# Two convolutions ahead: a convolution moved from a stage of its own into the loop over the queries

## The chip, the cores and the metric

The kernel runs on one core of one Trainium2 chip. The metric is the time of one execution on the device, in microseconds. Three runs of the kernel before gave 4277.91, 4282.75 and 4284.51 us; the median is 4282.75. One more execution was recorded by the hardware profiler.

## What is computed

The input x has 16 images of 256 channels and 64 x 64 pixels, in float32. Two layers follow one another, each added to its own input. Cut to what matters (B = 16, C = 256, N = 4096 tokens, nh = 8 heads of hd = 32):

```python
def layer0(x):                       # base_kernel [8, 32, 32, 3, 3]
    pooled = x.mean(axis=(2, 3))
    h = relu(pooled @ ap_w1.T + ap_b1)
    angles = tanh(h @ ap_w2.T + ap_b2) * (pi / 4)       # 8 a image
    w = rotate_bilinear(base_kernel, angles).reshape(B * C, 32, 3, 3)
    feat = conv2d(x.reshape(1, B * C, H, W), w, pad=1, groups=B * 8)
    m = relu(pooled @ meta_w1.T + meta_b1)
    return feat * sigmoid(m @ meta_w2.T + meta_b2)

def layer1(x):
    q, kv = xt @ Wq.T + bq, xt @ Wkv.T + bkv            # xt: tokens x 256
    q, k = ((relu(t) + 1e-6) / softplus(scale) for t in (q, k))
    q = q**3 / norm(q**3) * norm(q); k = k**3 / norm(k**3) * norm(k)
    z = 1 / (q . k.sum(tokens) + 1e-6)
    out = (q @ (k.T @ v)) * z                           # each head by itself
    out = out + depthwise_conv5x5(v) + dwc_b
    return (out @ Wproj.T + bproj).transpose(...)

x = x + layer0(group_norm(x))        # 32 groups of 8 channels
x = x + layer1(group_norm(x))
```

The weights of the convolution thus hang on the image: each image has its own eight angles, found from means over its pixels, and its own modulation of the channels.

## The kernel before

Each engine has its own program, written out by hand; semaphores tie them together (`wait_ge`, `then_inc`), and each engine does its instructions strictly in the order written. That order, and the order of the DMAs on SyncE (SP), is all that sets which work stands beside which. Matrices go through TensorE (PE) in pairs of float16 halves, a high one and a low one that holds the rest, in three products of four (`PASSES`).

An image b goes through these stages, in the function `batch` of each engine:

1. **Keys and values**, eight units of 512 tokens, each in two steps (`step_kv`): projection, the powers and norms of the keys, and the sum that makes the state of the attention. The change leaves it alone but for the small matmuls of `modulation`.
2. **Depthwise convolution**, `depthwise`: 32 channels of 9 matmuls each on PE, in four PSUM banks; ACT copies each one out (L1119). Beside it DVE takes the statistics of image b+2's pixels (`pixel_stats`, 16 BATCH_NORM_STATS), and ACT prepares the first three planes of image b+1 (`planes`, L1056: normalise in one pass, then set the borders to zero in six small ones).
3. **Convolution of image b+1**, `convolution`: eight groups of 32 channels (`GROUPS`), each in two halves of 512 columns (q = 0, 1), so 16 half groups, each of 12 matmuls (L1264). Half q goes to bank VA[q]. For a group, ACT makes the plane, DVE casts its high half (`high`), GpSimd (POOL) subtracts to get the low half. DVE then takes the bank, multiplies by the modulation and adds the residual (L792, in `conv_steps`), and takes the statistics for the second norm (L795); ACT adds the bias (`shift`), and SP stores the image x1 to memory. Between groups stand the small chains of image b+2's statistics: mean, deviation, angles. ACT ends them with `squash` (Tanh and Sigmoid, Sin), and POOL rotates the kernels in `rotation`, 27 chained operations.
4. **Queries' loop**, units u = 0 to 10, each in two steps p = 0, 1 (`step_q`). It is a pipeline: in step (u, p) PE does the projection of unit u (L1283), the transposes of the queries one step before (L1333), the attention of unit u-1 (L1342), the output projection of unit u-2 (L1361, h = 0 in bank PP and h = 1 in bank SM, both in step p = 1) and the transposes of the outputs (L1351). ACT does `squares`, `norms`, `sixths` (L1085), the copies of the transposed tiles (`transposed_q`, L1126; `high_out`, L1130). DVE does `floor_max` (L809), `ratio` (L820), `cube`, `denominators`, `inverses`, `quotients`, `low_out` (L899) and `finish` (L893). POOL adds the depthwise result to the quotients (L528). From u = 3 on, image b+1's attention inputs are prepared as well: ACT normalises (`attn_input`), DVE casts (L803), POOL subtracts. Units 3 to 7 have every one of these; unit 8 starts the keys of image b+1.

The body runs in a loop over images 0 to 13, then by itself for image 14 (no image b+2) and image 15 (nothing ahead). In front stands a prologue: loading and splitting of the weights, the statistics and the chain of image 0, its rotation, the convolution of image 0, its attention inputs, the first keys.

In the printed functions, L numbers are lines of the kernel before.

## Time and profile before

| | |
|---|---|
| median of three runs | 4282.75 us |
| profiled execution, its own time | 4280.34 us |
| its span, first to last instruction | 4278.5 us |
| PE busy | 3613.9 us, 84% of the span |
| DVE, ACT busy | 2916.5 us (68%), 2882.6 us (67%) |
| POOL busy | 1394.2 us, 33% |
| mean granted clock of PE | 0.971 of full speed |
| HBM traffic over the span | 113 GB/s |

PE is the busiest engine, and is named in 58% of the chain of work that ended last. A share of busy time is a mean over stages with different limits, so the rows below are taken stage by stage, from one image in the middle of the run (b = 1, with the convolution of image 2). In a window's row the columns are named; in a timeline's row, a bracket tells how long the engine was idle before the instruction and what released it. Engines: PE = TensorE, PEld = its weight loads, DVE = VectorE, ACT = ScalarE, POOL = GpSimd.

### The profile page before, as it was taken

What the parts mean: (1) busy time and instruction counts of PE and PEld (TensorE: products, weight loads), DVE (VectorE), ACT (ScalarE), POOL (GpSimd) and SP (SyncE); (2) the same over time, 40 slices, a digit from 0 to 9 for tenths busy, and PEclk for the clock granted to TensorE, in tenths of its full rate; (3) what the DMA queues carried; (4) which work ended last, traced back from release to release, by engine and by line L of the source; (5) the groups of instructions that cost most, each with busy time, mean ns of one, the idle gap of its engine ahead of it and who ended that gap; (6) DMA issues with size and microseconds to landing.
All of it is one profiled execution on the core that took longest, in us unless ns stands there. A gap on an engine that the chain in (4) does not pass through costs nothing.

```text
span 4278.5 us, 94152 instructions
## 1 busy us (share of the span) xinstructions
PE 3613.9 (84%) x26496; PEld 2725.6 (64%) x26496; DVE 2916.5 (68%) x7633; ACT 2882.6 (67%) x8141; POOL 1394.2 (33%) x1317
## 2 busy tenths in 40 slices
PE   0478898988889888898988889888898988889897
PEld 0265666757567575666757567675666757567686
DVE  6465767667576775867667576775857668585756
ACT  2366776767667676766767667676766767677675
POOL 0442522325143242513325143242513325142301
PEclk9989999999999999999999999999999999999999
DMA  4434434344443434444344442434444343432412
GB/s 161 135 95 149 131 116 126 109 131 126 132 132 95 139 107 140 131 122 123 112 126 126 141 135 89 135 116 129 130 131 121 105 132 118 150 111 81 129 40 69
DMA packets 558467, 516.39 MB, mean 121 GB/s; under 512 B 97296, under 2 KB 491664, under 8 KB 557712
## 3 DMA queue, kind: packets, MB, share of 16 engines
q1 hardware_dynamic: 557968, 510.53, 39.5%
q8 instruction: 217, 3.56, 0.4%
q14 instruction: 282, 2.31, 0.2%
HBM read 351.02 MB, written 134.22 MB: 113 GB/s over the span
## 4 chain that ended last, share of the span: by engine, by line
PE 58%; DVE 14%; issue 12%; ACT 9%; POOL 4%; DVEq 1%; DMA 1%; SPq 1%; ACTq 0%; POOLq 0%
PE VAB L1264 17%; PE F L1283 8%; PE VAB L1283 6%; PE F L1322 5%; PE T L1294 4%; PE PP L1361 4%; PE VAB L1322 4%; PE VAB L1342 4%; PE SM L1361 4%; POOL XR L528 4%; DVE XR L883 2%; ACT V L1119 2%; DVE WK L830 2%; ACT WK L1085 2%; ACT WK L1079 2%
## 5 line engine op out<-in xcount | busy, mean ns | idle before, releaser
L1283 PE MATMUL F<-WQ,XHL 128*128 128x256 f16 x6144 | 833.0, 277 | 45.7 <-DVE XR L792 13.7
L1264 PE MATMUL VAB<-WK,BD 128*128 128x512 f16 x3072 | 725.4, 396 | 106.2 <-DMA BD<-RHL 55.2
L528 POOL TENSOR_TENSOR XR<-XR,V 128x512 f32<-128x512 f32 x256 | 326.9, 1277 | 1334.0 <-DVE XR L883 1334.0
L1079 ACT ACTIVATE WK<-F,SCAL 128x256 f32<-128x256 f32 x1024 | 474.4, 469 | 396.0 <-DVE F L809 395.2
L511 POOL TENSOR_TENSOR WK<-XP,WK 128x1122 f16<-128x1122 f32 x128 | 289.8, 2265 | 1253.5 <-DVE WK L775 1253.5
L1283 PEld LDWEIGHTS F<-WQ,XHL 128*128 128x128 f16 (+1 forms) x6144 | 609.4, 100 | 131.3 <-issue 54.6
L1264 PEld LDWEIGHTS VAB<-WK,BD 128*128 128x128 f16 x3072 | 302.7, 101 | 495.5 <-issue 89.2
L1085 ACT ACTIVATE WK<-WK,SCAL 128x256 f32<-128x256 f32 x1024 | 513.1, 508 | 76.1 <-DVE WK L815 73.2
L1342 PE MATMUL VAB<-KVS,VT 128*128 128x132 f32 x2048 | 296.2, 289 | 197.6 <-POOL XR L528 197.5
L809 DVE TENSOR_TENSOR F<-F,FL 128x512 f32<-128x512 f32 x512 | 355.7, 695 | 108.4 <-PE F L1285 102.7
L1283 PE MATMUL VAB<-WQ,XHL 128*128 128x256 f16 x3072 | 407.0, 273 | 0.0
L1342 PEld LDWEIGHTS VAB<-KVS,VT 128*128 128x128 f32 x2048 | 256.9, 195 | 230.7 <-POOL XR L528 200.1
L815 DVE TENSOR_TENSOR WK<-WK,F 128x512 f32<-128x512 f32 x512 | 349.8, 683 | 71.0 <-ACT WK L1079 55.3
L792 DVE SCALAR_TENSOR_TENSOR XR<-VAB,MODC,XR 128x512 f32<-128x512 f32 x256 | 191.7, 749 | 244.6 <-PE VAB L1264 244.1
L1156 ACT ACTIVATE XR<-XR,BPC 128x1024 f32<-128x1024 f32 x128 | 147.0, 1148 | 305.9 <-DVE ST L795 305.8
L1294 PE MATMUL T<-VT,WK 128*128 128x129 f32 x2048 | 289.2, 285 | 69.3 <-DVE WK L830 63.4
L775 DVE CAST WK<-XP 128x1122 f16<-128x1122 f32 x128 | 97.4, 762 | 354.0 <-ACT XP L1064 289.4
L1283 PEld LDWEIGHTS VAB<-WQ,XHL 128*128 (+1 forms) x3072 | 301.3, 98 | 36.4
L519 POOL TENSOR_TENSOR XHL<-XP,XHL 128x512 f16<-128x512 f32 x256 | 290.6, 1136 | 94.1 <-DVE XHL L803 94.1
L1294 PEld LDWEIGHTS T<-VT,WK 128*128 128x128 f32 x2048 | 255.7, 196 | 98.3 <-DVE WK L830 92.9
L899 DVE SCALAR_TENSOR_TENSOR XR<-T,SCAL,XR 128x512 f16<-128x512 f32 x256 | 191.3, 747 | 179.2 <-ACT XR L1130 179.2
L1322 PE MATMUL F<-V,TP 128*128 128x248 f16 (+1 forms) x2304 | 294.8, 284 | 14.1 <-ACT V L1119 14.1
(185 smaller groups left out, 7242.5 us busy)
## 6 DMA issues: line engine op xcount, KB each, us to landing
XR<-xr SPq DMA_DIRECT2D x256, 512.0 KB, 4.9
XP<-xp SPq DMA_DIRECT2D x128, 561.0 KB, 3.8
x<-XR SPq DMA_DIRECT2D x512, 128.0 KB, 2.1
XP<-x SPq DMA_DIRECT2D x256, 256.0 KB, 3.3
XR<-x SPq DMA_DIRECT2D x256, 256.0 KB, 3.3
out<-XR SPq DMA_DIRECT2D x256, 256.0 KB, 3.1
BD<-RHL SPq DMA_DIRECT2D x256, 96.0 KB, 2.3
XHL<-toeplitz SPq DMA_DIRECT2D x2, 3072.0 KB, 12.9
```

The source lines that it names most:

```text
L519: g_.tensor_tensor(lo, U[:, u % 3, h].rearrange("p m y x -> p y m x"), hi, ALU.subtract).then_inc(l_rdy, 1)
L528: g_.tensor_tensor(o, o, fm, ALU.add).then_inc(o_rdy, 2)
L809: v.tensor_tensor(f, f, fl, ALU.max).then_inc(f_max, 1)
L815: v.tensor_tensor(K3[:, p, :], K2[:, p, :], F[p][:, :], ALU.mult).then_inc(f_cube, 1)
L1079: a.activation(K2[:, p, ts], F[p][:, ts], ACT.Square, scale=inv_a, accum_out=S2[:, 2 * p + t:2 * p + t + 1]).then_inc(f_sq, 1)
L1085: a.activation(K2[:, p, t * C:(t + 1) * C], K3[:, p, t * C:(t + 1) * C], ACT.Square, scale=inv_a, accum_out=S6[:, 2 * p + t:2 * p + t + 1] ...
L1264: ins = t_.matmul(VA[q], BD[:, j, HALVES * wa + h, sx, P * sy:P * (sy + 1)], SG[:, g % 3, xa, 16 * q + sy:16 * q + sy + 16, sx:sx + 32], s ...
L1283: t_.matmul(o, XHL[:, xa, h, at], WQ[:, wa, h, c0:c0 + C], start=(k == 0), stop=False)
L1294: ins = t_.matmul(T[h][:, 0:P + 1], K3[:, p, t * C + h * P:t * C + (h + 1) * P], VT[:, p, t, h, 0:P + 1], start=False, stop=False)
L1322: ins = t_.matmul(bank[:, lo:hi], TP[:, c, d, ta, :], V[:, c, va, lo + sh:hi + sh], start=(k == 0), stop=(k == 8))
L1342: ins = t_.matmul(VA[t][:, h * KVC:(h + 1) * KVC], QT[:, p, h, t * P:(t + 1) * P], KVS[:, h, :], start=True, stop=True)
L1361: ins = t_.matmul((PP, SM)[h][:, :], WP[:, wa, kk, h * P:(h + 1) * P], OT[:, xa, kk, :].rearrange("p (y m x) -> p m y x", y=4, m=4), start ...
```

## The change

The convolution runs two images ahead instead of one, and has no stage of its own any more. Its 16 half groups stand in the queries' loop of image b: half group 2u + p of image b+2 in step (u, p), for u = 0 to 7. All of them go to bank SM. The output projection, which used SM for h = 1, now has bank PP for both halves, one ahead of the convolution and one behind it. Attention no longer waits for POOL's addition but for DVE's quotients (`z_rdy` instead of `o_rdy`). On PE:

```diff
+            def convolve(c, g, q):
+                h, j = divmod(g, GPH)
+                n = 2 * (GROUPS * c + g) + q
+                if q == 0:
...
+                pe.wait_ge(x1_rdy, n + (1 if early(c) else X1_CR))
+                half = half_tile(c, g).rearrange("p a (r c) -> p a r c", c=PW)
+                k = 0
+                for wa, xa in PASSES:
+                    for sy in range(2):
+                        for sx in range(2):
+                            ins = t_.matmul(conv_bank(c, q)[:, :],
+                                            BD[:, j, HALVES * wa + h, sx, P * sy:P * (sy + 1)],
+                                            half[:, xa, 16 * q + sy:16 * q + sy + 16, sx:sx + 32],
+                                            start=(k == 0), stop=(k == 11))
+                            k += 1
+                ins.then_inc(conv_full, 1)
...
-                pe.wait_ge(o_rdy, 2 * (b * PAIRS + 2 * u + p) + O_CR)
+                pe.wait_ge(z_rdy, 4 * (b * PAIRS + 2 * u + p) + Z_CR)
                 for t in range(2):
                     for h in range(HALVES):
...
-            def step_q(b, u, p, live):
+            def step_q(b, u, p, live, conv):
                 if live(p):
                     pe.wait_ge(f_cube, b * 2 * PAIRS + PAIRS + 2 * u + p + 1)
                     project(b, u, p, F, 0)
                 if live(p - 1):
                     transpose_q(b, u - 1 + p, 1 - p)
+                if p == 1 and live(-4):
+                    output(b, u - 2, 0)
+                if conv and u < GROUPS:
+                    convolve(b + 2, u, p)
                 if live(p - 2):
                     attention(b, u - 1, p)
                 if p == 1 and live(-4):
-                    for h in range(HALVES):
-                        output(b, u - 2, h)
+                    output(b, u - 2, 1)
                 if live(p - 3):
                     transpose_o(b, u - 2 + p, 1 - p)
```

DVE takes a half group out of the bank one step later (k = 2u + p - 1), as the third piece of its step, and its order within a step is new; ACT prepares the next group's plane at the end of step p = 0, and the shift at the end of p = 1:

```diff
-            def step_q(b, u, p, live, nxt, keys=False, fresh=False):
+            def step_q(b, u, p, live, nxt, keys=False, conv=False):
                 n = b * 2 * PAIRS + PAIRS + 2 * u + p
+                k = 2 * u + p - 1
+                if live(p) or keys:
+                    floor_max(n, p)
                 if live(p - 4):
                     low_out(b, u - 2, p)
-                if live(p) or keys:
-                    floor_max(n, p)
+                if conv and 0 <= k < 2 * GROUPS:
+                    conv_out(b + 2, k)
                 if live(p - 1):
                     ratio(n - 1, 1 - p, S6, S2)
...
+                if conv and 0 <= k < 2 * GROUPS:
+                    result_stats(b + 2, k)
+                if p == 1 and live(-4):
+                    finish(b, u - 2, 0)
+                if p == 0 and live(-6):
+                    finish(b, u - 3, 1)
+                if nxt:
+                    attn_input(b + 1, u - 3, p, False)
+                if conv and p == 1 and u + 1 < GROUPS:
+                    high(b + 2, u + 1)
                 if live(p) or keys:
                     cube(n, p)
                 if live(p - 2):
+                    denominators(b, u - 1, p)
                     inverses(b, u - 1, p)
-                if live(p - 2):
-                    quotients(b, u - 1, p, fresh and u == 1 and p == 0)
-                if nxt:
-                    attn_input(b + 1, u - 3, p, False)
+                    quotients(b, u - 1, p)
...
-            def step_q(b, u, p, live, nxt, keys=False):
+            def step_q(b, u, p, live, nxt, keys=False, conv=False):
                 n = b * 2 * PAIRS + PAIRS + 2 * u + p
-                if p == 0 and live(-4):
-                    high_out(b, u - 2, 0)
+                if live(p - 4):
+                    high_out(b, u - 2, p)
                 if live(p) or keys:
                     squares(n, p)
...
+                    transposed_q(b, u - 1 + p, 1 - p)
                     norms(n - 1, 1 - p, den_eps)
...
-                if p == 0 and live(-3):
-                    high_out(b, u - 2, 1)
                 if live(p) or keys:
                     sixths(n, p)
+                if conv and p == 0 and u + 1 < GROUPS:
+                    planes(b + 2, u + 1)
+                if conv and p == 1 and 1 <= u <= GROUPS:
+                    shift(b + 2, u - 1)
```

The planes, which had three buffers, have one (PL); the half precision planes have two (SL), the pixels of the residual two (X2, apart from XR). To make room, the attention inputs have two buffers instead of three, and ROT and RHL share memory with X2. What SP does in a step of the loop is therefore written out as well:

```diff
+            def step(b, u, p, s1, s2):
+                if p == 0:
+                    if s2 and 2 <= u < GROUPS:
+                        pixels_after(b + 2, u)
+                    if 3 <= u < NU + 3:
+                        store(b, u - 3, 1)
+                else:
+                    if 2 <= u < NU + 2:
+                        store(b, u - 2, 0)
+                    if 3 <= u <= NU:
+                        load_residual(b, u - 1)
+                        if s1:
+                            next_unit(b + 1, u - 1)
+                    if s2 and 1 <= u <= GROUPS:
+                        store_x1(b + 2, u - 1)
+                    if s2 and u + 2 < GROUPS:
+                        planes_after(b + 2, u + 2, GROUPS * (b + 2) + u + 2)
```

In the depthwise stage the statistics now are those of image b+3. DVE first does the chain of the second norm of image b+1 (`chain_1`), then the statistics and the chain of b+3; the small matmuls stand between PE's channels, and the roots between ACT's copies; `squash` stands behind ACT's last copy, ahead of the queries' loop, and only the first plane (group 0) is prepared here:

```diff
+                if s1:
+                    chain_1(b + 1)
+                    checked(1)
+                if s3:
+                    for g in range(GROUPS):
+                        pixel_stats(b + 3, g)
+                    deviations(b + 3, 0)
+                if s2:
+                    high(b + 2, 0)
+                if s3:
+                    chain_0(b + 3)
+                    checked(0)
+                for u in range(NU + 3):
                     for p in range(2):
...
-            def depthwise(b, last):
+            def depthwise(b, ahead):
                 for c in range(HD):
                     act.wait_ge(dw_full, b * HD + c + 1)
                     a.activation(FM[:, c, :], DW[c % 4][:, 0:NT * HEADS], ACT.Identity, scale=fm_fac,
                                  bias=DWB[:, c:c + 1]).then_inc(fm_rdy, 1)
-                    if not last and c in (20, 24, 28):
-                        planes(b + 1, (c - 20) // 4)
+                    if ahead >= 1 and c == 7:
+                        root(b + 1, 1)
+                    if ahead >= 2 and c == 11:
+                        planes(b + 2, 0)
+                    if ahead >= 3 and c == 20:
+                        root(b + 3, 0)
+                if ahead >= 3:
+                    squash(b + 3)
...
+                    if ahead >= 1 and c == 3:
+                        group_mean(b + 1, 1)
+                    if ahead >= 1 and c == 5:
+                        group_spread(b + 1, 1)
+                    if ahead >= 3:
+                        if c == 17:
+                            group_mean(b + 3, 0)
+                        if c == 19:
+                            group_spread(b + 3, 0)
+                        if c == 24:
+                            patch_mean(b + 3)
+                        if c == 27:
+                            hidden(b + 3)
+                        if c == 30:
+                            heads(b + 3)
```

PE's queue for the loop opens with waits for the chain's end, for the norm and for the weights (`zb_rdy`, `norm_rdy[1]`, `wt_in`). The body runs for images 0 to 12 in the loop (`ahead` = 3), and by itself for images 13, 14 and 15 (`ahead` = 2, 1, 0), without the parts that belong to images past the last.

The prologue now has the statistics, chains, rotations and convolutions of two images (0 and 1) and the statistics of image 2. Its order is another: the taps of the 3 x 3 kernels and the pixels are loaded first; the splitting of the attention's weights stands between the half groups of convolution 0, and attention inputs between those of convolution 1. The grid of shifts is an input now instead of being made on the chip.

The excerpts below give the order of the instructions, with each kernel's own line numbers. First PE in step p = 1 of a steady unit, before: the transposes of the queries (MATS), attention (KVS), the two outputs (WP) and the transposes of the output.

```order
L1333 MATMUL T<-MATS,WK 128x128 x4
L1339 ISA
L1342 MATMUL VAB<-KVS,VT 128x132 x4
L1357 ISA
L1361 MATMUL PP<-XR,WP 128x512 x6
L1357 REGISTER_ALU
L1361 MATMUL SM<-XR,WP 128x512 x6
L1351 MATMUL T<-MATS,XR 128x128 x4
```

The same place after the change:

```order
L1555 MATMUL T<-MATS,K 128x128 x4
L1579 ISA
L1583 MATMUL PP<-XR,WP 128x512 x6
L1470 REGISTER_ALU
L1476 MATMUL SM<-SL,BD 128x512 x12
L1561 ISA
L1564 MATMUL VAB<-KVS,VT 128x132 x4
L1579 REGISTER_ALU
L1583 MATMUL PP<-XR,WP 128x512 x6
L1573 MATMUL T<-MATS,XR 128x128 x4
```

One output has moved ahead of the attention, and the 12 matmuls of a half group stand between them. Next, ACT from the end of step (u, 0) into (u, 1), before: the sixth powers, the copy of the transposed output of the step before, and the squares of the next step.

```order
L1085 ACTIVATE WK,S<-WK,SCAL 128x256 x2
L1129 REGISTER_ALU
L1130 ACTIVATE XR<-T,SCAL 128x2x256
L1074 REGISTER_ALU
L1076 ISA
L1079 ACTIVATE WK,S<-F,SCAL 128x256 x2
```

After the change:

```order
L1283 ACTIVATE K,S<-K,SCAL 128x256 x2
L286 ISA
L1253 ACTIVATE PL<-PL,PR 128x1122
L1255 REGISTER_ALU
L1259 ACTIVATE PL<-PL 64x34 x2
L1262 ACTIVATE PL<-PL 32x32 x4
L1333 REGISTER_ALU
L1334 ACTIVATE XR<-T,SCAL 128x2x256
```

The seven passes of a plane stand behind the sixth powers now, and the copy `high_out` behind them. Last, DVE in step (u, 0), from the start of the step, before: `low_out` (L899), `floor_max`, `ratio`, `finish` (L893).

```order
L803 CAST XHL<-XP 128x512
L899 SCALAR_TENSOR_TENSOR XR<-T,SCAL,XR 128x2x256
L806 REGISTER_ALU
L809 TENSOR_TENSOR F<-F,FL 128x512
L819 REGISTER_ALU
L820 RECIPROCAL RATIO<-S 128x2
L821 REGISTER_ALU
L823 TENSOR_SCALAR RATIO<-S,RATIO 128x1 x2
L890 REGISTER_ALU
L893 SCALAR_TENSOR_TENSOR XR<-SM,SCAL,XR 128x512
```

After the change:

```order
L949 TENSOR_TENSOR F<-F,FL 128x512
L1036 SCALAR_TENSOR_TENSOR XR<-T,SCAL,XR 128x2x256
L930 SCALAR_TENSOR_TENSOR RX<-SM,MODC,RX 128x512
L959 REGISTER_ALU
L960 RECIPROCAL RATIO<-S 128x2
L961 REGISTER_ALU
L963 TENSOR_SCALAR RATIO<-S,RATIO 128x1 x2
L935 REGISTER_ALU
L936 BN_STATS ST<-RX 128x6
```

`floor_max` has moved ahead of `low_out`, `conv_out` (L930) has come in third, and its statistics (L936) behind the ratio.

## Rows read from the trace of the kernel before

**Rows 1.** Windows: us; busy us of PE, PEld, DVE, ACT, POOL; clock; DMA share.

```profile
572.03:608.58 36.55, 32.47 (x290) 28.52 (x289) 15.15 (x44) 25.93 (x54) 5.62 (x3) 0.97 0.43 147
608.58:655.31 46.73, 45.80 (x206) 20.56 (x207) 30.17 (x58) 26.16 (x51) 12.49 (x6) 0.96 0.55 162
655.31:686.10 30.79, 22.77 (x165) 18.20 (x166) 21.05 (x74) 19.55 (x63) 4.54 (x4) 0.94 0.37 103
686.10:740.48 54.38, 47.32 (x363) 37.63 (x361) 44.87 (x120) 40.02 (x120) 22.64 (x20) 1.00 0.43 127
740.48:762.65 22.17, 17.32 (x114) 11.64 (x112) 17.32 (x36) 14.49 (x37) 11.23 (x12) 0.92 0.48 141
```

**Rows 2.** Timeline, PE, unit 5: start us, us, engine, line, operation, out<-in.

```profile
714.69 1.17 PE L1342 MATMUL VAB<-KVS,VT 128*128 128x132 f32 x8 [1.41 <-POOL XR L528]
715.70 1.46 PE L1361 MATMUL PP<-XR,WP 128*128 128x512 f16 x6
...
718.72 0.82 PE L1283 MATMUL F<-WQ,XHL 128*128 128x256 f16 x6
```

**Rows 3.** Timeline, DVE, the same unit.

```profile
717.72 0.42 DVE L803 CAST XHL<-XP 128x512 f16<-128x512 f32 x1
...
719.64 0.75 DVE L899 SCALAR_TENSOR_TENSOR XR<-T,SCAL,XR 128x512 f16<-128x512 f32 x1 [1.51 <-ACT XR L1130]
720.45 0.70 DVE L809 TENSOR_TENSOR F<-F,FL 128x512 f32<-128x512 f32 x1
...
721.50 0.74 DVE L893 SCALAR_TENSOR_TENSOR XR<-PP,SCAL,XR 128x512 f32<-128x512 f32 x1
```

**Rows 4.** Timeline, PE, four half groups of the convolution.

```profile
621.15 10.84 PE L1264 MATMUL VAB<-WK,BD 128*128 128x512 f16 x48
```

**Rows 5.** Timeline, DVE, beside the convolution.

```profile
616.55 0.74 DVE L792 SCALAR_TENSOR_TENSOR XR<-VAB,MODC,XR 128x512 f32<-128x512 f32 x1
617.32 0.69 DVE L795 BATCH_NORM_STATS2 ST<-XR 128x6 f32<-128x512 f32 x1
```

**Rows 6.** Timeline, ACT, the steady unit.

```profile
712.67 0.69 ACT L1130 ACTIVATE XR<-T,SCAL 128x512 f16<-128x512 f32 x1
713.24 0.52 ACT L1085 ACTIVATE WK<-WK,SCAL 128x256 f32<-128x256 f32 x1
```

**Rows 7.** Timeline, ACT, two planes, one right behind the other.

```profile
607.88 1.32 ACT L1056 ACTIVATE XP<-XP,PR 128x1122 f32<-128x1122 f32 x1
...
610.83 1.32 ACT L1056 ACTIVATE XP<-XP,PR 128x1122 f32<-128x1122 f32 x1
```

**Rows 8.** Timeline, ACT, one of the table loads of squash.

```profile
646.07 1.28 ACT L1042 ACT_TABLE_LOAD   x1
```

**Rows 9.** Windows, a stretch of the tail.

```profile
745.50:750.70 5.20, 3.38 (x14) 1.85 (x15) 5.02 (x15) 4.46 (x15) 2.49 (x3) 0.79 0.74 217
```

**Rows 10.** Timeline, PE, in that stretch.

```profile
747.32 1.17 PE L1342 MATMUL VAB<-KVS,VT 128*128 128x132 f32 x8 [1.85 <-POOL XR L528]
748.32 2.59 PE L1361 MATMUL PP<-XR,WP 128*128 128x512 f16 x6
```

**Rows 11.** Timeline, PE, depthwise channels in pairs.

```profile
575.11 2.09 PE L1322 MATMUL VAB<-V,TP 128*128 128x256 f16 x18
577.03 2.09 PE L1322 MATMUL F<-V,TP 128*128 128x256 f16 x18
```

**Rows 12.** Timeline, DVE, statistics beside the depthwise stage.

```profile
574.45 4.84 DVE L769 BATCH_NORM_STATS2 ST<-XR 128x6 f32<-128x512 f32 x8
...
586.75 0.17 DVE L694 COPY GS<-MV 128x8 f32<-128x8 f32 x1
```

**Rows 13.** Timeline, PE, the prologue.

```profile
158.53 6.87 PE L1264 MATMUL VAB<-WK,BD 128*128 128x512 f16 x24 [55.22 <-DMA BD<-RHL]
...
244.56 1.46 PE L1283 MATMUL F<-WQ,XHL 128*128 128x256 f16 x6 [11.13 <-DVE WK L815]
```

**Rows 14.** Timeline, POOL, the first rotation.

```profile
109.93 0.24 POOL L470 TENSOR_TENSOR TT<-XX,SIN 128x36 f32<-128x36 f32 x1 [59.89 <-issue]
```

1060 lines of the change are left out of this document (603 added, 457 removed).

## The prediction

> **What bounds the kernel now.** I read the stages first, then one unit of each stage, engine by engine. [rows 1] cut one image in the middle of the run (the others repeat it): depthwise 36.55 us, convolution 46.73, the queries' loop 30.79 (units 0 to 2) + 54.38 (units 3 to 7) + 22.17 (tail) = 107.34, together 190.6 us. The keys' and values' loop, which makes up the rest of an image, is left as it is by the change. Look at PE's share: 45.80 of 46.73 us in the convolution, 47.32 of 54.38 in the steady units. A steady unit lasts 54.38/5 = 10.88 us, has 9.46 us of PE work, and its one gap is 1.41 us, ended by GpSimd's addition [rows 2]. DVE has a gap of its own each unit, ended by ACT's copy L1130 [rows 3]. So PE is nearly full, and a gain must come from its gaps, some 7 us in the steady units, 8 in units 0 to 2, 5 in the tail and 4 in the depthwise stage.
>
> **The change, a steady unit.** The convolution's own stage goes (46.73 us), and its 16 half groups go into units 0 to 7, one per step. A half group is 12 matmuls; 48 take 10.84 us [rows 4], so 12 take 2.69 and a unit gets 5.37. By work alone a unit would be 9.46 + 5.37 = 14.83 us, against 10.88 + 46.73/8 = 16.72 us for the same work now. But three waits stand in the new order.
> First, the half groups all go to the one bank SM (before: two banks), so PE may start half group k only when DVE's conv_out of k-1 is done, and that stands third in DVE's step, behind floor_max of this step's projection. Second, output of half 0 stands ahead of the convolution and needs low_out of the same step, behind ACT's high_out. Third, ACT's high_out of step (u,1) stands behind sixths and planes of (u,0).
> Count from the start of PE's projection in (u,0). DVE's floor_max starts 1.73 us later (718.72 to 720.45, [rows 2, 3]). On DVE an instruction starts some 0.09 before the end of the one ahead, so floor_max takes 0.61 and with the ratio 1.05 (720.45 to 721.50), low_out 0.66, conv_out 0.66 (or 0.77 to its dependant, [rows 5]), the statistics 0.60, finish 0.66 and the cast 0.33: cube starts at 5.69 and ends at 6.4. ACT's sixths, two passes with a read each, take 1.0 [rows 6]: 7.4. planes take 2.95 (607.88 to 610.83, [rows 7]): 10.35. high_out 0.69: 11.05; low_out 0.75: 11.8; PE 11.9. Then output, convolution, attention, output, transposes: 1.01 for attention and 3.02 for the two outputs and the transposes (2 x 1.30 + 0.43) from [rows 2], 2.69 for the convolution: 18.6 us. Meanwhile PE's own way through (u,0) is 3.85 (conv_out) + 2.69 + 1.01 + 0.43 = 8.0, and (u,1) without the planes would be 3.2 + 6.7 = 9.9: 17.9. So a unit is 18.6 us with planes (units 3 to 6), 17.9 without (unit 7), where the work needs 14.83. Units 3 to 7 come to 4 x 18.6 + 17.9 = 92.3. Queued behind: conv_out holds up DVE's cube and quotients, high_out holds ACT's squares of the next step; both are done before PE asks again.
> **Fill and tail.** In unit 0 ACT first does squash(b+3), three table loads of 1.28 us [rows 8] and five short operations, 4.7 us; in the old order this lay beside the convolution. The load for Sqrt follows as before. ACT's chain squash 4.7, squares 0.9, cube 0.8, sixths 1.0, planes 2.95, squares, copy, norms with the load, sixths 3.9, squares and cube wait 1.8, sixths 1.0, planes 3 to 3.5, then squares, cube, sixths and the shift 4.4 gives 24.5 us for units 0 and 1; unit 2, with no casts and one finish less, is 17.9. Together 42.3 against 30.79 now, with 6 half groups in it (16.1 us of PE). The tail has no convolution: 22.5 (22.17 now; its output has one bank instead of two).
> Loop: 42.3 + 92.3 + 22.5 = 157.1 us.
> **The clock.** PE's granted clock falls from 2.4 to 1.2 GHz now and then: after a gap of 1.85 us at 745.5, [rows 9] give 0.79 over the stretch and the six output matmuls take 2.59 us instead of 1.46 [rows 10, 2]. The 1.41 us gaps do not do it (1.00 over units 3 to 7, [rows 1]). In the new unit PE is ready for the next piece 1.97 us into each step (9.46 less two outputs of 1.30, two attentions of 1.01 and two transposes of 0.43, halved), so it has two gaps: 3.85 - 1.97 = 1.9 and 11.9 - 8.0 - 1.97 = 1.9. From nothing up to some 1.2 us lost in every unit; I take 1.7 an image. Loop 158.8, against 107.34 + 46.73 = 154.07: +4.7.
> **Depthwise.** Today 32 channels at about 0.96 us (two from 575.11 to 577.03, [rows 11]), 30.8 in all, a slow start of 1.2, and stalls for three planes. New: the chain for the norm of b+1 comes first on DVE, and its Sqrt stands behind ACT's channel 7, which ends near 572.03 + 1.2 + 8 x 0.96 + 0.9 = 581.8; some 14 small operations at 0.2 follow (a copy is 0.17, [rows 12]): 584.8. Only then come the 16 statistics of b+3 and their aggregation, which take 12.3 us now (574.45 to 586.75, [rows 12]), waits for the DMA included: 597.1. PE asks for that mean after channel 17, near 591.3. It stalls 5.8 us, and restarts at the lower clock (1.2). The stage then is 30.8 + 1.2 + 0.3 (one planes) + 1.6 (ten small matmul groups) + 5.8 + 1.2 + 0.8 for the last copy = 41.7, with 0.7 for the second chain's hold-ups 42.4: +5.8 on 36.55.
> **The sum.** Thirteen images run the whole body: 13 x (4.7 + 5.8) = +137. Image 13 has no statistics to wait for, no squash: about -1. Image 14 has no convolution: -46.7, and the depthwise stage 3 shorter; its loop, with no squash ahead of it, is near 107.34 - 4.7 = 102.6: -46.7 - 3 = -50. Image 15: 0.
> Prologue: the first convolution starts at 158.53, after 55.22 us of waiting for the weights, and steady work on the keys at 244.56 [rows 13]. From the rotation's first operation (109.93, [rows 14]) to the weights is 48.6 us. The new order starts the statistics as soon as constants have landed: 48.6 + 12.3 + chains and loads of some 27 us (from 0 to 45) puts convolution 0 at 88; the second rotation paces it and its weights follow, 65 us; convolution 1, 50; chains and squash, 9: keys at 212. So -32, between -70 (no chain in the way) and +5 (each rotation in full on the path).
> Total: 137 - 1 - 50 - 32 = +54 on the profiled execution's 4280.34 (span 4278.5): 4334. The median shown is 2.4 above that execution, so I say 4336 us, +1.2%.
> The Trainium skill, Perfetto Trace Analysis, Optimizing Tensor Performance, says that independent matmul groups should rotate through different PSUM banks, so that one's evacuation overlaps the next one's matmuls. The change does the reverse for the convolution; the trace agrees as far as it goes, with 45.80 of 46.73 us busy on two banks.
>
> **Rivals.**
> A, faster: the waits overlap better than laid out, and the unit comes near PE's work. For it: today's unit comes to 87% of it with a wait on GpSimd that the change removes (attention now waits for DVE's quotients, not for the addition behind them). If units 2 to 7 take 16.0 (half way from 14.83), the loop is 15 us shorter, the image 4.6 below now: 13 x -4.6 - 83 = 4137; with the stall in the depthwise stage and 17.2 a unit it is 4240. Against: each wait is a data dependency, not a matter of rates. The same skill page, Optimization Strategy, says that interleaving regimes with different busiest engines may help; by that rule alone the unit would be 14.83 and the time near 4060, which no row here shows.
> B, no change: breaking even needs +6.4 an image instead of +10.5, as when statistics are in time for channel 22, say: 4283.
> C, slower than forecast, the clock: if each of units 2 to 7 loses 1.7 us, the image costs 8.5 more: 4445. Point of decision: gaps of 1.85 us or more in most units; it happened once at 1.85, not at 1.41.
> D, SyncE: in (u,1) it issues stores, residual, unit and four x1 stores, then the next planes into a single buffer. If these land after sixths (7.4 us into the unit), all waits: about 1 us a unit, 4420.
>
> **How the numbers follow.** Forecast (order of waits as laid out) 0.48, A 0.27, B 0.10, C 0.10, D 0.05. A change under 0.2% can't be told from none here (about 9 us). Faster: A and a little of the forecast's lower side, 0.29. Same 0.11. Slower 0.60. The forecast's own range is 4285 to 4400 (0.5 us a unit either way is 40 us in all, the stall 0 to 8 us an image, the prologue 35). To leave out no more than 0.2, the range goes down into A: 4205 to 4430.
>
> **What would show it.** In the changed profile: units of 18 to 19 us with two gaps on PE, ended by conv_out and by low_out (if they are 15 to 16, A); DVE's low_out waiting for ACT behind planes; about 6 us of PE idle in mid depthwise, ended by DVE's mean; a loop of 155 to 162 us; keys of image 0 in steady work near 212. Wrong if the gaps are under 1 us, or if the planes' DMA ends most waits.

## The result

| | us |
|---|---|
| before, median of 4 runs | 4282.51 (4277.91 to 4284.51) |
| after, median of 4 runs | 4594.52 (4585.6 to 4597.3) |
| ratio, 95% interval | 1.0728 (1.0713 to 1.0743) |
| forecast | 4336 (4205 to 4430) |

The change makes the kernel 7.3% slower; slower was forecast, but 1.2%, and the time lies above the range. The span grew by 317.0 us, from 4278.5 to 4595.5. Laid along the starts of the depthwise stage (PE's first L1322 of an image, L1529 in the changed kernel), image by image, this comes to:

| part | before | after | difference | forecast |
|---|---|---|---|---|
| start to image 0's depthwise stage | 315.2 | 379.7 | +64.5 | -32 |
| one of the images 0 to 12 (mean) | 255.97 | 278.09 | +22.1, thirteen times +287.6 | +10.5, +137 |
| image 13 | 254.0 | 253.6 | -0.4 | -1 |
| image 14 | 246.4 | 210.5 | -35.9 | -50 |
| image 15 and the end | 135.2 | 136.5 | +1.3 | 0 |

### The profile page after: what moved, and what is told of

Read it like the earlier page. It is cut to its first block, busy times and chain, and to the rows that moved or that the text cites. A ratio compares the mean times of both kernels' runs of the same rounds, so it can differ in the third digit from the quotient of the medians.

```text
span 4595.5 us, 93402 instructions
## 1 busy us (share of the span) xinstructions
PE 3722.2 (81%) x26496; PEld 2757.3 (60%) x26496; DVE 2924.1 (64%) x7587; ACT 2916.5 (63%) x8129; POOL 1440.0 (31%) x1320
## 4 chain that ended last, share of the span: by engine, by line
PE 48%; DVE 18%; ACT 12%; issue 11%; DMA 6%; SPq 2%; POOL 1%; DVEq 1%; ACTq 0%; POOLq 0%
PE PP L1583 8%; PE F L1490 8%; PE SM L1476 7%; PE VAB L1490 5%; PE VAB L1529 5%; PE F L1529 4%; PE T L1501 4%; DVE XR L1036 3%; DMA PL<-xp 3%; ACT PL L1253 3%; PE VAB L1564 2%; ACT K L1283 2%; DVE K L955 2%; ACT PL L1262 2%; DVE ST L914 2%
## 5 line engine op out<-in xcount | busy, mean ns | idle before, releaser
L1490 PE MATMUL F<-WQ,XHL 128*128 128x256 f16 x6144 | 819.5, 275 | 27.6 <-ACT V L1317 19.4
L1476 PE MATMUL SM<-SL,BD 128*128 128x512 f16 x2688 | 685.9, 407 | 178.9 <-DVE RX L930 170.4
L1283 ACT ACTIVATE K<-K,SCAL 128x256 f32<-128x256 f32 x1024 | 513.2, 505 | 450.7 <-DVE K L955 448.7
L1277 ACT ACTIVATE K<-F,SCAL 128x256 f32<-128x256 f32 x1024 | 473.5, 469 | 274.0 <-DVE F L949 272.0
L1583 PE MATMUL PP<-XR,WP 128*128 128x512 f16 x1536 | 430.2, 422 | 251.5 <-DVE XR L1036 235.7
L635 POOL TENSOR_TENSOR XHL<-U,XHL 128x512 f16<-128x512 f32 x256 | 315.0, 1234 | 935.3 <-DVE XHL L943 935.3
L1476 PEld LDWEIGHTS SM<-SL,BD 128*128 128x128 f16 x2688 | 265.7, 103 | 558.7 <-DVE RX L930 195.3
L955 DVE TENSOR_TENSOR K<-K,F 128x512 f32<-128x512 f32 x512 | 347.8, 679 | 52.2 <-ACT K L1277 52.2
L1501 PE MATMUL T<-VT,K 128*128 128x129 f32 x2048 | 290.4, 286 | 71.4 <-DVE K L970 63.4
L1529 PE MATMUL F<-V,TP 128*128 128x248 f16 (+1 forms) x2304 | 293.5, 285 | 2.9 <-ACT V L1317 2.9
L1529 PE MATMUL VAB<-V,TP 128*128 128x248 f16 (+1 forms) x2304 | 292.0, 284 | 0.0
L1492 PE MATMUL F<-BQ,ONES 128*128 128x256 f16 x1024 | 281.2, 275 | 0.0
```

What stands on the lines that cost most here:

```text
L635: g_.tensor_tensor(lo, U[:, u % 2, h].rearrange("p m y x -> p y m x"), hi, ALU.subtract).then_inc(l_rdy, 1)
L955: v.tensor_tensor(K3[:, p, :], K2[:, p, :], F[p][:, :], ALU.mult).then_inc(f_cube, 1)
L1277: a.activation(K2[:, p, ts], F[p][:, ts], ACT.Square, scale=inv_a, accum_out=S2[:, 2 * p + t:2 * p + t + 1]).then_inc(f_sq, 1)
L1283: a.activation(K2[:, p, t * C:(t + 1) * C], K3[:, p, t * C:(t + 1) * C], ACT.Square, scale=inv_a, accum_out=S6[:, 2 * p + t:2 * p + t + 1] ...
L1476: ins = t_.matmul(conv_bank(c, q)[:, :], BD[:, j, HALVES * wa + h, sx, P * sy:P * (sy + 1)], half[:, xa, 16 * q + sy:16 * q + sy + 16, sx: ...
L1490: t_.matmul(o, XHL[:, xa, h, at], WQ[:, wa, h, c0:c0 + C], start=(k == 0), stop=False)
```

## The profile after

First the stages of one image, as [rows 1] show them of before: image 1's depthwise stage, units 0 to 2, units 3 to 7, the tail, and unit 5 alone. The columns are those of [rows 1].

```profile
659.88:704.77 44.89, 36.55 (x308) 31.51 (x307) 23.18 (x90) 21.17 (x42) 2.32 (x1) 0.89 0.33 108
704.77:746.76 41.99, 36.19 (x233) 23.48 (x233) 25.27 (x59) 33.10 (x92) 10.87 (x7) 1.00 0.21 60
746.76:845.22 98.46, 81.01 (x483) 51.07 (x480) 61.25 (x144) 58.45 (x153) 34.70 (x25) 0.93 0.51 152
845.22:871.93 26.71, 17.58 (x114) 12.25 (x112) 18.10 (x39) 16.34 (x38) 10.86 (x11) 0.93 0.50 153
787.18:807.38 20.20, 16.53 (x98) 10.30 (x96) 12.41 (x29) 12.22 (x32) 7.46 (x6) 0.92 0.55 164
```

Depthwise, convolution and loop took 36.55 + 46.73 + 107.34 = 190.6 us in [rows 1]; they take 44.89 + 167.16 = 212.0 now. The granted clock is the thing to see: 1.00 in units 3 to 7 of before, 0.93 here, and 0.92 in unit 5, which lasts 20.2 us. The clock stands at 2.4 GHz but for a piece at 1.2. That unit on PE (the timeline's rows that answer to [rows 2]):

```profile
790.98 2.85 PE L1476 MATMUL SM<-SL,BD 128*128 128x512 f16 x12 [1.67 <-DVE RX L930]
...
799.13 1.88 PE L1583 MATMUL PP<-XR,WP 128*128 128x512 f16 x6 [2.01 <-DVE XR L1036]
800.80 4.11 PE L1476 MATMUL SM<-SL,BD 128*128 128x512 f16 x12
...
805.65 1.46 PE L1583 MATMUL PP<-XR,WP 128*128 128x512 f16 x6
```

Both gaps of the forecast are there: one ended by conv_out (L930), one by low_out (L1036). Behind the second the clock falls: six output matmuls take 1.88 us, not 1.46, and a half group's twelve 4.11, not 2.85. It does so in 42 of the 52 units 3 to 6 of images 0 to 12. ACT and DVE in the same unit show the chain that was laid out, cube (L955) on DVE, the plane (L1253 and on) and high_out (L1334) on ACT, and low_out on DVE:

```profile
794.57 1.31 ACT L1253 ACTIVATE PL<-PL,PR 128x1122 f32<-128x1122 f32 x1
...
797.51 0.69 ACT L1334 ACTIVATE XR<-T,SCAL 128x512 f16<-128x512 f32 x1
```

```profile
792.86 0.68 DVE L955 TENSOR_TENSOR K<-K,F 128x512 f32<-128x512 f32 x1
...
798.23 0.75 DVE L1036 SCALAR_TENSOR_TENSOR XR<-T,SCAL,XR 128x512 f16<-128x512 f32 x1 [0.81 <-ACT XR L1334]
```

The forecast put cube, plane, high_out and output at 5.69, 7.4, 10.35 and 11.9 us into the unit; from the unit's start at 787.18, cube starts at 5.68, the plane at 7.39, high_out at 10.33 and output at 11.95. Starts of PE's projections, averaged over thirteen images, give the units: 10.0, 14.0, 19.3, then 19.8, 20.3, 20.1, 19.6, and 17.6 for unit 7. Where the clock does not fall a unit takes 18.5; where it falls once, 20.2. The length of the gap alone does not decide it: with the same second gap of 2.0 us the clock falls in units 3 to 6 of image 1 and stays up in units 3 and 6 of image 4, and in image 13, with gaps of 1.75 and 1.84, it stays up in all four.

In the depthwise stage, PE and the DVE rows it waits for:

```profile
686.61 0.59 PE L1433 MATMUL SM<-GS,MATS 128*128 128x8 f32 x2 [6.89 <-DVE GS L839]
687.05 3.91 PE L1529 MATMUL VAB<-V,TP 128*128 128x256 f16 x18
```

```profile
685.63 0.71 DVE L834 BATCH_NORM_AGGREGATE MV<-ST 128x2 f32<-128x12 f32 x8
686.38 0.17 DVE L839 COPY GS<-MV 128x8 f32<-128x8 f32 x1
```

PE stops for 6.89 us at channel 18, and the next two channels take 3.91 us where two took 2.09 [rows 11]. Last the prologue: convolution 0 begins and ends its first stretch, convolution 1 begins, the keys begin.

```profile
108.98 10.56 PE L1476 MATMUL VAB<-V,BD 128*128 128x512 f16 x36 [9.70 <-DMA BD<-RX]
...
196.69 5.30 PE L1476 MATMUL VAB<-V,BD 128*128 128x512 f16 x12 [4.22 <-DVE XR L930]
209.20 0.59 PE L1458 MATMUL SM<-MODM,MATS 128*128 128x8 f32 x2 [7.21 <-DVE MODM L897]
223.63 6.93 PE L1476 MATMUL VAB<-V,BD 128*128 128x512 f16 x24 [13.84 <-DMA BD<-RX]
...
300.98 1.44 PE L1490 MATMUL F<-WQ,XHL 128*128 128x256 f16 x6
```

Convolution 0 starts 49.5 us earlier than in [rows 13], but takes 93 us (108.98 to 201.99) instead of some 50 (158.53 to 209.4), with PE waiting 32.4 us in all for DVE between half groups. The keys start at 300.98 us, not 224.37, and run steadily from 309.4, not 244.56. Between the convolutions, the second rotation's last operation on POOL and the weights' DMAs on SP stand far apart:

```profile
170.82 5.12 POOL L621 TENSOR_TENSOR RX<-RX 128x192 f16<-128x192 f32 x6 [0.18 <-POOL RX L615]
```

```profile
211.57 10.41 SPq L382 DMA_DIRECT2D BD<-RX  x16
```

The weights were ready at 176 us. SP sends them only when convolution 0 has done its last matmul (`weights` waits for `conv_full`, and there is one buffer BD) and behind the last stores of x1.

## The experiments

All start from the changed kernel. Each was run beside the kernel before on the same chip. Experiments 1 to 8 and 12 are one execution each; four executions of the changed kernel lay within 12 us, so a smaller difference in the total says nothing by itself. "An image" is the mean of images 0 to 12.

**1. Keep PE busy in the gap.** The clock or a wait?

```diff
                 if p == 1 and live(-4):
+                    pe.wait_ge(y_rdy, (b * NU + u - 2) * HALVES + Y_CR)
+                    for _ in range(7):
+                        t_.matmul(PP[:, :], WP[:, 0, 0, 0:P], WQ[:, 0, 0, 0:512], start=True, stop=True)
                     output(b, u - 2, 0)
```

> Seven matmuls of 128x512 whose result is thrown away are put into bank PP ahead of output 0, in PE's wait for low_out. If the clock is what lengthens most steady units from 18.6 to 20.2 us (theory C: PE falls to half clock once a unit because of its two waits), it stays up: units 3 to 6 at 18.6 us, and with four of six falls in the loop gone, some 6 us an image less: near 4595 - 13 x 6 = 4515. Rival W: the 1.6 us are a wait (a DMA, say) and the low clock only goes with it: units stay at 20.2 and the time near 4595, or above by the seven matmuls (1.5 us a unit, 4700) if they are in the way.

Measured 4525.0 us, 70 less, with 896 more matmuls. The windows of unit 3 and of units 4 to 7 of image 1:

```profile
738.91:757.38 18.47, 16.40 (x105) 10.54 (x103) 12.31 (x29) 12.21 (x32) 7.40 (x6) 1.00 0.46 138
757.38:830.70 73.32, 65.40 (x414) 42.19 (x412) 48.70 (x115) 46.27 (x121) 27.16 (x20) 1.00 0.58 169
```

The clock is 1.00 and the units are 18.5 (means 18.5 to 18.7, unit 7 17.9). So the 1.7 us above 18.5 is the clock, and the clock falls because of PE's idle time in the gap: the chain of waits is still there, since the units are no shorter than 18.5. This is rival C's mechanism. It is worth 70 us, not the whole of what the forecast missed.

**2. high_out ahead of the plane** (ACT). Is the plane on the chain?

```diff
-                if live(p - 4):
-                    high_out(b, u - 2, p)
+                if p == 0 and live(-4):
+                    high_out(b, u - 2, 0)
...
                     sixths(n, p)
+                if p == 0 and live(-3):
+                    high_out(b, u - 2, 1)
                 if conv and p == 0 and u + 1 < GROUPS:
                     planes(b + 2, u + 1)
```

> ACT copies the transposed output of unit u-2 (high_out, second half) ahead of the plane in step (u,0), not behind it. If the chain of waits runs floor_max, cube, sixths, plane, high_out, low_out, output (theory of the prediction), the plane leaves it: low_out of (u,1) then waits for its floor_max alone, output starts 0.8 us earlier, and a unit takes 17.8 us at full clock instead of 18.6. Rival: the plane is not on the chain (PE's two gaps come from the bank SM alone); units unchanged at 18.6.

Measured 4441.1 us, 153 less. The window of unit 3, and PE's two waits in unit 4:

```profile
730.59:748.24 17.65, 14.89 (x99) 9.87 (x96) 12.35 (x29) 12.05 (x32) 6.68 (x5) 1.00 0.49 144
```

```profile
752.03 2.84 PE L1478 MATMUL SM<-SL,BD 128*128 128x512 f16 x12 [1.67 <-DVE RX L930]
...
759.27 1.47 PE L1585 MATMUL PP<-XR,WP 128*128 128x512 f16 x6 [1.10 <-DVE XR L1036]
```

The second gap shrinks from 2.01 to 1.10 us, every unit from 2 on takes 17.64, and at gaps of 1.67 and 1.10 the clock stays at 1.00. The theory of the prediction holds to 0.2 us. The chain gave 0.8 us a unit (18.46 to 17.64); not losing the clock gave more (units 3 to 6: 79.9 to 70.6, of which 3.3 is the chain).

**3 and 4. conv_out first in DVE's step, alone and with experiment 2.** Do PE's gaps add?

```diff
+                if conv and 0 <= k < 2 * GROUPS:
+                    conv_out(b + 2, k)
                 if live(p) or keys:
                     floor_max(n, p)
                 if live(p - 4):
                     low_out(b, u - 2, p)
-                if conv and 0 <= k < 2 * GROUPS:
-                    conv_out(b + 2, k)
```

> DVE takes the half group out of bank SM first in its step, ahead of floor_max and low_out. PE's gap ahead of the convolution goes (1.67 us in step p = 0). If the two gaps simply add up, a unit takes 18.6 - 1.7 = 16.9 us at full clock. If the chain through ACT (cube, sixths, plane, high_out) sets the unit, PE only waits longer for output 0: 18.6 less the 0.7 by which DVE's cube comes earlier, 17.9 us. A third: the residual's pixels, asked for one step before, are not there yet, and DVE waits for the DMA: no gain.

> Both moves. By the theory of the prediction each alone leaves the other's wait: together PE's step (u,0) ends at 6.3 us, high_out at 7.5, floor_max and low_out at 9.4, and the unit takes 16.2 us at full clock, with gaps of 1.3 us in all, so that the clock stays up: 4 x (20.2 - 16.2) + 1.4 for unit 7 = 17 us an image less, near 4370. If only the bank matters, as e3; if only ACT's order, as e2.

Measured 4593.4 and 4533.4 us; the second expectation missed by 160 us. In the first the gap ahead of the convolution is gone, but output 0 waits 5.1 and 3.5 us in two units of image 1, up to 6.4 over the run. Where nothing else interferes its units take 18.2, between the 17.9 of the chain and 18.6; they are not 16.9, so the gaps do not add. In the second, unit 3 is as forecast and unit 4 is not:

```profile
743.66:759.49 15.83, 14.72 (x99) 9.93 (x96) 11.98 (x30) 11.02 (x32) 5.86 (x5) 1.00 0.49 147
759.49:781.46 21.97, 16.94 (x98) 10.47 (x96) 12.56 (x30) 12.95 (x33) 9.03 (x7) 0.84 0.56 163
```

One row of what DVE waited for in the second kernel, over the whole run (total us, times, longest):

```profile
DVE RX L930 <- DMA RX<-xr: 176.4, 69, 4.6
```

The first kernel has 171.8 us of it. The pixels of a new group are asked for in (u, 0) and wanted first thing in (u, 1). They were not there: the third case of the first expectation, no gain, is what came. The changed kernel has no such row: its conv_out came late enough.

**5. conv_out first in p = 0 only,** with experiment 2; there it is the second half of a group whose pixels have long been loaded.

```diff
+                if conv and p == 0 and 0 <= k < 2 * GROUPS:
+                    conv_out(b + 2, k)
                 if live(p) or keys:
                     floor_max(n, p)
                 if live(p - 4):
                     low_out(b, u - 2, p)
-                if conv and 0 <= k < 2 * GROUPS:
+                if conv and p == 1 and 0 <= k < 2 * GROUPS:
                     conv_out(b + 2, k)
```

> As the run with ACT's high_out ahead of the plane, and DVE takes the half group out of SM first in its step in p = 0 only (there it is the second half of a group whose pixels have been in memory for a step; in p = 1, where e4_both waited up to 4.6 us for the DMA of the new group's pixels, conv_out stays third). Theory: e4's units of 20 to 22 us came from that DMA wait alone; without it the unit is 16.2 to 16.5 us and the clock stays up: 5 x 1.2 = 6 us an image under e2_high's 4441, near 4360. Rival: the pixels land 11.8 us into the unit, so they end a wait wherever conv_out stands in p = 1 once the unit is under some 17 us: units stay at 17 to 17.6 or alternate, 4420 to 4500.

Measured 4340.5 us, 101 less than experiment 2. Units 2 and 3 of image 1 and then 4 to 6:

```profile
707.60:723.52 15.92, 14.82 (x99) 9.85 (x96) 12.23 (x30) 11.50 (x31) 5.12 (x5) 1.00 0.41 120
723.52:739.32 15.80, 14.70 (x98) 9.93 (x96) 11.99 (x30) 10.99 (x32) 5.84 (x5) 1.00 0.55 160
739.32:789.61 50.29, 44.64 (x290) 29.55 (x288) 37.26 (x88) 36.70 (x97) 23.04 (x16) 1.00 0.67 191
```

PE has 14.7 us of work in a unit of 15.8, the price by work alone being 14.83 in the prediction. Units 2, 3 and 7 are at 15.8 to 16.1, a little under the theory's 16.2 to 16.5; units 4 to 6 take 16.7 to 17.3, near the rival's 17 to 17.6. The total fits the theory. DVE's waits for pixels are down to 87.7 us in 61 times; that these hold units 4 to 6 is likely, but no run shows it. The prediction weighed the rule of the Trainium skill (Perfetto Trace Analysis, Optimizing Tensor Performance) that independent groups of matmuls should rotate through PSUM banks. Here the order of the reader on DVE closed the 1.67 us gap with the one bank kept; no run tried a second bank for the convolution.

**6. Statistics between the pieces of the norm's chain** (DVE, depthwise stage), with experiment 2.

```diff
-                if s1:
+                if s3:
+                    deviations(b + 1, 1)
+                    pixel_stats(b + 3, 0)
+                    pixel_stats(b + 3, 1)
+                    spreads(b + 1, 1)
+                    pixel_stats(b + 3, 2)
+                    pixel_stats(b + 3, 3)
+                    variance(b + 1, 1)
+                    pixel_stats(b + 3, 4)
+                    pixel_stats(b + 3, 5)
+                    scale_and_bias(b + 1, 1)
+                    checked(1)
+                    pixel_stats(b + 3, 6)
+                    pixel_stats(b + 3, 7)
+                    deviations(b + 3, 0)
+                elif s1:
                     chain_1(b + 1)
                     checked(1)
-                if s3:
-                    for g in range(GROUPS):
-                        pixel_stats(b + 3, g)
-                    deviations(b + 3, 0)
```

> As e2_high, and in the depthwise stage DVE does image b+3's statistics between the pieces of the chain for b+1's norm instead of behind the whole chain; PE's small matmuls stand where they did. Theory (order of waits): statistics are done 16 us into the stage instead of 26.5, PE's stop of 6.9 us ahead of channel 18 shrinks to about 1, and the clock does not fall behind it: 44.1 us from the stage's start to the queries' loop becomes 36 to 38, 13 x 7 = 90 us, near 4350. Rival: the end of the chain (angles) or the weights for b+2 then hold up PE at the loop's start instead: under 2 us an image.

Measured 4338.1 us, 103 less than experiment 2.

```profile
635.95:671.58 35.63, 33.12 (x309) 29.48 (x307) 22.16 (x90) 21.13 (x42) 2.32 (x1) 1.00 0.43 136
```

The stage is 35.6 us instead of the changed kernel's 44.9, at clock 1.00, under the 36.55 of [rows 1]. PE's stop of 6.9 us is gone, and did not come back at the loop's start.

**7 and 12. The prologue: the taps' DMA, then DVE's part of them.** In 7, ten of the twelve loads of taps are dropped; in 12 the low halves are made for 2 of 128 columns as well, with a clearing of them at the start (both with experiment 2).

```diff
-                    if 1 <= g <= 5:
-                        load_taps(2 * g)
-                        load_taps(2 * g + 1)
...
-                act.wait_ge(taps_in[i % 2], 16 * (i // 2 + 1))
+                act.wait_ge(taps_in[i % 2], 16)
...
+            setup(v.memset(TPM[:, :, 1, :], 0.0))
...
-                hi, lo = (TPM[:, 8 * i:8 * i + 8, a, :] for a in range(2))
+                hi, lo = (TPM[:, 8 * i:8 * i + 8, a, 0:2] for a in range(2))
```

> As e2_high, and in the prologue only the first two of the twelve chunks of depthwise taps are loaded; the other ten are cast and split from those again, so the depthwise result is not the reference's. DVE's and ACT's work is the same, ten DMAs and their waits are gone. If the round trip of the chunks through two buffers (DMA 6.4 us, ACT, DVE, next DMA) is what makes convolution 0 last 93 us where before it lasted 50, this is 25 to 35 us shorter: near 4410. If it is DVE's own work between the half groups (12 x 3 us of taps, some 25 of splitting), under 10 us: 4432 or more.

> As e7_taps (only two chunks of taps are loaded), and DVE makes the low half of two columns of a chunk only, so that 12 x 3 us of its work between the half groups of convolution 0 go as well; the depthwise result is not the reference's. A clearing of the low halves, some 13 us, stands at DVE's start. If DVE's own work is what is left of the pace of convolution 0 (75 us in e7, 93 after the change, 50 before), it comes to 45 to 55 us and the first depthwise matmul some 20 us earlier, less up to 10 for the clearing. If ACT's planes or POOL's second rotation set it, it stays at 70 to 75.

Measured 4423.1 and 4417.0 us. Convolution 0 goes from 91 us in experiment 2 (93 in the changed kernel) to 74 (107.54 to 181.8) and to 69 (108.27 to 177.6), the first depthwise matmul from 377.2 us in experiment 2 to 355.8 and 347.7. Neither expectation held: in the start of the first depthwise stage the round trip was worth 21 us and DVE's taps another 8 (5 in convolution 0; the totals of 7 and 12 differ by 6). The first half groups of experiment 12 show what is left:

```profile
108.27 9.67 PE L1476 MATMUL VAB<-V,BD 128*128 128x512 f16 x36 [9.71 <-DMA BD<-RX]
121.74 4.41 PE L1476 MATMUL VAB<-V,BD 128*128 128x512 f16 x12 [3.80 <-DVE XR L928]
130.57 5.08 PE L1476 MATMUL VAB<-V,BD 128*128 128x512 f16 x12 [4.42 <-DVE XR L928]
138.18 4.48 PE L1476 MATMUL VAB<-V,BD 128*128 128x512 f16 x12 [2.53 <-DVE XR L928]
...
153.25 24.35 PE L1476 MATMUL VAB<-V,BD 128*128 128x512 f16 x96 [3.65 <-DVE XR L928]
```

```profile
122.33 1.01 DVE L806 TENSOR_SCALAR XHL<-XHL,SCAL 128x768 f32<-128x768 f32 x1
123.37 1.39 DVE L807 CAST XHL<-XHL 128x768 f16<-128x768 f32 x1
124.80 2.04 DVE L808 TENSOR_TENSOR XHL<-XHL 128x768 f16<-128x768 f32 x1
126.87 1.19 DVE L812 COPY BQ<-XHL 1x768 f16<-1x768 f16 x1
128.09 1.54 DVE L813 COPY BQ<-XHL 1x768 f16<-1x768 f16 x1
129.67 0.75 DVE L928 SCALAR_TENSOR_TENSOR XR<-VAB,MODC,XR 128x512 f32<-128x512 f32 x1
```

Up to 153 us PE's gaps of 2.5 to 4.4 us stand where DVE splits a bias or a weight ahead of conv_out (7.3 us here, 122.33 to 129.67); with the big splits done, the last 96 matmuls run without a gap. That the splits make up the rest is read from these rows; no kernel without them was run.

**8. Two banks and the old order where there is no convolution** (units 8 and 9; images 14, 15), with experiment 2. Its core on DVE:

```diff
+                if not conv or u > GROUPS:
+                    if live(-6):
+                        finish(b, u - 3, p, (PP, SM)[p])
```

> As e2_high, and wherever PE has no convolution (units 8 and 9 of each image, images 14 and 15) the output projection goes back to the order and banks of before: attention first, then both outputs, in PP and SM, and DVE's finish one unit later. If the single bank and DVE's finish in the same step are what make units of image 14 take 12.7 to 14.1 us instead of 10.8, and the tail of every image 5 us longer, image 14 gets 20 us shorter and the others 3 to 5 each: near 4441 - 20 - 50 = 4370. Rival: the tail is longer by the shift, the last conv_out and the clock: image 14 gains, the others do not: 4420.

Measured 4436.0 us, 5 less, too little to be told from none. Image 14 takes 202.0 us instead of 211.7, its units 3 to 7 last 11.6 instead of the 12.7 to 14.1 of the changed kernel: there bank and order cost 10 us. The tail of the other images as a whole does not change (92.6 us from unit 8 to the next depthwise stage, 92.6 in experiment 2, 87.4 before). But the trace shows that the edit moved a wait there. Steady keys begin 24.9 us after the start of unit 8, not 27.1 (mean of images 1 to 12; 22.9 before), and one unit of keys later the difference is gone (32.3 and 32.2; 27.6 before). With DVE's finish one unit later, SP's store of the output goes out later, and the last attention input behind it is asked for 18.3 us into unit 8 instead of 14.9 (image 1). ACT waits for it, and PE for ACT:

```profile
845.18 1.52 ACT L1271 ACTIVATE U<-U,PR 128x512 f32<-128x512 f32 x2 [7.85 <-DMA U<-x]
```

```profile
850.25 1.97 PE L1506 MATMUL T<-VT,K 128*128 128x129 f32 x8 [3.10 <-ACT VT L1304]
```

ACT's waits for these inputs are 117.6 us in all, 24.1 in experiment 2. So this run does not tell how much of the tail's 5 us is the bank and the order. What makes them longer stays open.

**9 and 10. Everything that helped, and the shift earlier.** Experiment 9 is 2, 5, 6 and 8 together; 10 moves ACT's shift in p = 1 ahead of the sixth powers:

```diff
+                if conv and p == 1 and 1 <= u <= GROUPS:
+                    shift(b + 2, u - 1)
                 if live(p) or keys:
                     sixths(n, p)
...
-                if conv and p == 1 and 1 <= u <= GROUPS:
-                    shift(b + 2, u - 1)
```

> The edits of e5_conv0, e6_dw and e8_two together. If they act on different waits they add up: per full image 259.6 - 8.4 = 251.2 us against 256.0 of before; 13 x -4.8 = -62, prologue +62, image 13 -15, image 14 -44 (202.0 against 246.4): some 4280 - 60 = 4220. If they share a limit (the clock, the DMA queue), 4240 to 4280.

> As e9_all, and ACT's shift of a finished group stands ahead of the sixth powers in p = 1, where ACT waits 2.3 us for DVE's cube, not behind them: x1's store and with it the next pixels go out 1 us earlier. If the pixels' DMA is what still makes units 4 to 6 take 16.7 to 17.2 us where units 3 and 7 take 15.8, they come to 16.0: 3 x 0.9 x 13 = 35 us, near 4185. If it is the clock, no change (4215 to 4225).

Measured 4226.8 us (4 runs), ratio to before 0.9857 (0.9838 to 0.9876), and 4218.5 (2 runs), 0.9844 (0.9824 to 0.9864). The edits add up to within 7 us: an image takes 252.7 us. Between 9 and 10 the difference is too small to be told from none, and the 35 us that 10 was to bring did not come; its units 4 to 6 stayed at 16.7 to 17.1, so the pixels were not brought in early enough by it, or were not the limit. The waits for the attention inputs that experiment 8 brought are in both (121.5 and 120.9 us). Both beat the kernel before, by 1.4 and 1.6%.

**11. squash behind the loop,** with experiment 9's edits.

```diff
-                if ahead >= 3:
-                    squash(b + 3)
...
                         step_q(b, u, p, alive(u), s1 and u >= 3, s1 and u == NU, s2)
+                    if u == NU + 1 and ahead >= 3:
+                        squash(b + 3)
```

> As e9_all, and squash(b+3) stands behind ACT's step (9,1), not ahead of (0,0). By the prediction's account its 4.7 us of table loads lie on the path of units 0 and 1 (24.1 us where it was 15.7): units 0 and 1 take 19 to 20 us, 13 x 4 = 52 us less, near 4170. Rival: what is late then is the convolution's bank and the planes, or the keys of the next image wait for ACT instead: under 1 us an image.

Measured 4464.7 us, 238 more. Units 0 and 1 became 1.3 us shorter, not 4 to 5. ACT's table loads, in experiment 9 and here (columns: busy us, mean ns):

```profile
L1305 ACT ACT_TABLE_LOAD x14 | 18.0, 1283 | 0.3
```

```profile
L1305 ACT ACT_TABLE_LOAD x99 | 127.0, 1283 | 1.8
L1293 ACT ACT_TABLE_LOAD x98 | 125.7, 1283 | 8.3 <-DVE F L949 6.9
```

ACT now loads a table for the norms and one for the squares in each pass of the keys' loop: 183 more of 1.28 us, 235 us, which is about the loss. From unit 8 to the next depthwise stage an image takes 111.2 us instead of 93.6. Image 0's keys pay it too, though no moved squash runs ahead of them (the first depthwise stage starts at 398.4 us instead of 378.7): the loads stand in the body of the loop in the program as built. That they stand there because the loop can be entered with the table that squash leaves is the likely reason, and no run tests it.

**13. x1's stores first in SP's step,** with experiment 10's edits.

```diff
+                    if s2 and 1 <= u <= GROUPS:
+                        store_x1(b + 2, u - 1)
                     if 2 <= u < NU + 2:
                         store(b, u - 2, 0)
...
-                    if s2 and 1 <= u <= GROUPS:
-                        store_x1(b + 2, u - 1)
```

> As e10_shift, and SP issues the stores of x1 in p = 1 ahead of the output's store, the residual and the next unit, so that the next pixels are asked for earlier. DVE's waits for these pixels (75.8 us in 52 times in e10_shift) go, units 4 to 6 fall from 16.4-17.4 to about 16, and the time from 4218 to some 4190. If the queue's transfers themselves are the limit there (189 GB/s in these units), the wait moves to the residual or the attention's inputs: 4210 to 4225.

Measured 4331.7 us (5 runs), ratio to before 1.0121 (1.0103 to 1.0139), 113 worse than experiment 10. DVE's waits for pixels, in 10 and in 13:

```profile
DVE RX L930 <- DMA RX<-xr: 75.8, 52, 2.2
```

```profile
DVE RX L930 <- DMA RX<-xr: 151.5, 53, 4.3
```

And the queue's own:

```profile
SPq L262 <- ACT RX L1380: 140.2, 16, 10.7
```

```profile
SPq L262 <- ACT RX L1380: 991.2, 112, 12.3
```

SP now stands still for ACT's shift with the residual, the next unit and the next plane queued behind. ACT's waits for its planes rise from 43.3 to 155.3 us, units 4 to 6 take 20.6, 19.5 and 18.9 us, and the clock falls in two of them an image. Rival D's mechanism is thus shown, in an order that the change did not have: there ACT waits 30.3 us for planes in the whole run.

## Why the prediction was wrong

The forecast had 54 us for the span, and 317 came. Of the 263 us between them the prologue is 97 and image 14 is 14; over the thirteen full images the tail is 65, the clock 49, the depthwise stage 24 and units 0 to 2 13.

- **The order of waits in a unit: right.** 18.6 us was forecast for a unit with a plane, 17.9 without; 18.5 and 17.6 were measured where the clock held. Experiment 2 moved one link of the chain and the unit followed by 0.8 us.
- **The clock: the term was sized too small, and its condition was read too narrowly.** "I take 1.7 an image": it was 5.5 in units 3 to 6 (79.9 against 74.4), 3.2 falls an image in units 3 to 7. Rival C had the price a unit right (1.7) and its chance, 0.10, too low. The two gaps were forecast at 1.9 and 1.9 us, which is over the 1.85 us behind which [rows 9] show a fall, and rival C named this very bound; the forecast still took the milder case. "It happened once at 1.85" was also a misreading: in unit 2 of the same image the clock fell behind two gaps of 1.57 and 1.67 us, and attention took 1.99 us instead of 1.17. Experiment 1 shows the cause by itself.

```profile
676.63 1.99 PE L1342 MATMUL VAB<-KVS,VT 128*128 128x132 f32 x8 [1.67 <-POOL XR L528]
```

- **The prologue: the largest error of one term, +64.5 against -32.** The step "the second rotation paces it and its weights follow, 65 us" failed. From convolution 0 to convolution 1 it took 114.7 us. The rotation itself took what was forecast (109.2 to 175.9 us), but it did not pace: the weights followed convolution 0's end, and convolution 0 took 93 us. In experiment 7, with convolution 0 17 us shorter than in experiment 2, convolution 1 starts 22 us earlier. The steady keys, forecast at 212, came at 309.4: 21 us for the start of convolution 0 (109, not 88), 50 for this step, 12 for convolution 1 (62, not 50) and 15 behind it. What made convolution 0 long was the taps' round trip through two buffers (17 us of it, experiment 7), DVE's part of the taps (5, experiment 12) and, as far as the rows tell, the splitting of weights that DVE had got between the half groups. The instructions moved there were not counted one by one.
- **The depthwise stage: right in kind, 2 us short.** PE stopped where forecast, 6.9 us instead of 5.8, and lost 1.8 behind it at the lower clock. Experiment 6 removed both.
- **The tail: wrong.** 22.5 us was forecast for 22.17 before; it takes 26.7, and from unit 8 to the next image's depthwise stage 5.3 us more on average. The added cost was put at 0.3. Experiment 8 brought back the two banks and gained nothing as a whole, but delayed a load by it; the cause is open.
- **Image 14: the sign right, 14 us too much.** 10 of them are the output's order and bank (experiment 8), which I had put at nothing. The rest is open.

By image: fill +1.0, units 3 to 6 +5.5, unit 7 -0.3, tail +5.0, less the 1.7 allowed for the clock, make 9.5 of the 9.7 us by which the loop exceeds the forecast.

Rival A failed as the change stood, but not its idea: with the order mended, a unit takes 15.8 us at best, near the work in it, and with the depthwise stage and the output's order mended too the whole runs 1.4 to 1.6% faster than before. Rival B's case, statistics in time, came only with experiment 6.
